# A delta-rule attention stage in 32 software-pipelined tiles: the order of its four engines rewritten

## The reference, cut to what matters

```python
xn = _ln(_layernorm(h), ln_in_g, ln_in_b)
k = xn @ Wk.T + 0.1 * modifier(xn)   # the same for v and q; modifier: 192 -> 48, gelu, -> 768
k, v, q = _ln(each, per head of 64)  # 12 heads
for t in range(64):                  # M: 64 x 64 per batch and head, 0 at first
    out_t = M @ q_t
    kn = k_t / (norm(k_t) + 1e-6)
    pred = M @ kn
    coef = pred + lr * (pred - v_t)
    M = M - outer(coef, kn)
h = h + sigmoid(x @ Wg.T + bg) * (out @ Wo.T)
h = h + _ln(Wo @ (W2 @ relu(W1 @ _layernorm(h))))   # the feed-forward part with its own Wo; biases left out
```

## Time and profile before

| | us |
|---|---|
| median of 3 runs | 1397.5 (1397.04 to 1405.56) |
| the profiled execution | 1401.61 |
| its span | 1399.8 |
| PE busy | 1234.2 (88%) |
| DVE busy | 816.8 (58%) |
| ACT busy | 625.8 (45%) |
| POOL busy | 612.0 (44%) |

### The profile page before, as it was taken

One profiled execution on the slowest core, in us unless ns is written; L12 is line 12 of the kernel. 1 busy time (PEld: TensorE's weight loads), 2 busy tenths in 40 slices (PEclk: granted clock), 3 DMA queues, 4 the chain that ended last, 5 costly groups with the idle time before them and its releaser, 6 DMA issues.

```text
span 1399.8 us, 45227 instructions
## 1 busy us (share of the span) xinstructions
PE 1234.2 (88%) x17572; PEld 1007.1 (72%) x17572; DVE 816.8 (58%) x2152; ACT 625.8 (45%) x1539; POOL 612.0 (44%) x721
## 2 busy tenths in 40 slices
PE   3879999999996569999999989999998999999874
PEld 3846666666664458788788878887887888888763
DVE  0173333333333246778768777876877777787652
ACT  0002222222222345666656656655665665666532
POOL 0000000000000364776677667567666766766621
PEclk9989999999997668999999999999999999999987
DMA  8859999999990001111111111111111111111110
GB/s 304 297 220 342 379 364 371 382 371 370 379 362 14 12 12 22 28 28 25 31 28 29 25 30 29 25 34 28 25 27 30 31 24 31 26 25 25 28 22 19
DMA packets 176410, 169.82 MB, mean 121 GB/s; under 512 B 118198, under 2 KB 146425, under 8 KB 175609
## 3 DMA queue, kind: packets, MB, share of 16 engines
q1 hardware_dynamic: 176234, 167.37, 37.0%
HBM read 154.72 MB, written 12.58 MB: 120 GB/s over the span
## 4 chain that ended last, share of the span: by engine, by line
PE 34%; POOL 32%; issue 17%; DVE 9%; DMA 3%; SPq 2%; ACT 2%; POOLq 0%; DVEq 0%; ACTq 0%
PE PS L435 29%; POOL region L1093 10%; POOL region L1074 4%; POOL region L1079 3%; POOL xr_lo L1098 2%; POOL region L1087 2%; POOL region L1050 2%; POOL region L1085 1%; POOL region L1054 1%; PE PS L504 1%; POOL region L1069 1%; POOL region L1057 1%; POOL region L1064 1%; PE PS L674 1%; DVE region L1447 1%
## 5 line engine op out<-in xcount | busy, mean ns | idle before, releaser
L435 PE MATMUL PS<-region 64*64 64x64 f32 (+5 forms) x5936 | 366.2, 288 | 46.5 <-DMA region<-in_w 23.2
L435 PEld LDWEIGHTS PS<-region 64*64 64x64 f32 (+3 forms) x5936 | 244.6, 140 | 145.1 <-issue 100.9
L1093 POOL TENSOR_TENSOR region<-region,powers 128x24 f32<-128x24 f32 x64 | 212.6, 3322 | 5.0
L1020 POOL TENSOR_TENSOR region<-region,powers 128x1 f32<-128x1 f32 x32 | 6.1, 192 | 417.5 <-DVE region L1201 417.5
L684 PE MATMUL PS<-region 64*64 64x64 f32 x4608 | 162.7, 226 | 2.3 <-ACT region L923 2.1
L684 PEld LDWEIGHTS PS<-region 64*64 64x64 f32 x4608 | 149.5, 141 | 21.0 <-issue 17.2
L1317 DVE TENSOR_REDUCE region<-region 128x12 f32<-128x768 f32 x96 | 91.0, 948 | 126.0 <-ACT region L895 126.0
L435 PE MATMUL PS<-cw_hi,xr_hi 128*128 128x512 f32 (+3 forms) x384 | 140.5, 366 | 10.0 <-POOL xr_lo L1098 10.0
L435 PE MATMUL PS<-cw_lo,xr_hi 128*128 128x512 f32 (+3 forms) x384 | 132.5, 345 | 0.0
L435 PE MATMUL PS<-cw_hi,xr_lo 128*128 128x512 f32 (+3 forms) x384 | 131.7, 343 | 0.0
L674 PE MATMUL PS<-region 64*64 64x64 f32 x3072 | 64.7, 232 | 63.8 <-DVE region L1336 31.4
...
## 6 DMA issues: line engine op xcount, KB each, us to landing
...
n_scratch<-region SPq DMA_DIRECT2D x256, 12.0 KB, 1.6
region<-i_scratch SPq DMA_DIRECT2D x256, 12.0 KB, 1.8
```

What stands on the lines that cost most here:

```text
L435: return nc.tensor.matmul(dst, lhsT, rhs, start=first, stop=last)
L1093: pool.tensor_tensor(rs[:, cols], rs_var[:, cols], root[:, cols], ALU.pow).then_inc(S["rs_ready"], 1)
```

## The change

It rewrites the order in the loops of all five engines, and some of what is in them:

- PE: `read_out` goes from the end of step k to the head of the next; only piece 0 stands ahead of `key_norms` and `grams`; `weigh_out` comes behind these; the pieces 3, 4 and 5 stand between links of the solve, with `gates` and the feed-forward part near the end. The PSUM banks are dealt anew (`PIECE_BANK`): pieces 3 to 5 use bank 7, which `weigh_out` fills too, so piece 3 now waits for `gated_ready`.
- ACT: the keys' squares come before `turned_out`, `mean_square(m)` behind piece 0.
- `head_rstds` takes k, q and v one by one (12 columns each) and has lost its multiplication by 1/64, which `squares` now does.
- v's sums, root and scaling (m = 2) are done at the head of the next step, as j.
- `low_part` moves from POOL to DVE.
- The inversion is done in one go at the end of DVE's step.
- `gather_blocks` stores n whole, in two DMAs of 64 partitions x 12 heads x 256 bytes, so that the diagonal blocks lie at a constant pitch, and reads them back as 96 x 16 runs of 64 bytes; before, it stored eight times 16 x 12 runs of 64 bytes and read 96 runs of 1 KB. On SP it comes before `store_result`.

```diff
+PIECE_BANK = (0, 1, 0, 7, 7, 7)
...
-                for b in range(NBLK):
-                    at = b % BPS * BLK
-                    sp.dma_start(n_dram[b].rearrange("h t j -> t h j"),
-                                 nmat[j % 2][b * BLK:b * BLK + BLK, :, at:at + BLK]).then_inc(S["n_stored"], 16)
-                sp.wait_ge(S["n_stored"], (j + 1) * NBLK * 16)
+                for e in range(2):
+                    rows = bass.AP(n_dram.tensor, e * BPS * BLK_PITCH, [[SEQ, SEQ], [HEAD_PITCH, HEADS], [1, SEQ]])
+                    sp.dma_start(rows, nmat[j % 2][64 * e:64 * e + 64, :, :]).then_inc(S["n_stored"], 16)
+                sp.wait_ge(S["n_stored"], (j + 1) * 32)
                 need(sp, "d_ready", j)
                 settled(sp)
-                sp.dma_start(blocks[:, :, :], n_dram.rearrange("b h t j -> (b h) t j")).then_inc(S["gather_done"], 16)
+                diagonal = bass.AP(n_dram.tensor, 0, [[BLK_PITCH, NBLK * HEADS], [SEQ, BLK], [1, BLK]])
+                sp.dma_start(blocks[:, :, :], diagonal).then_inc(S["gather_done"], 16)
...
+                if live(x + 2):
+                    need(sp, "x_ready", x + 1)
+                    settled(sp)
+                    load_h(hp, "hp_in", x + 2)
+                if live(j):
+                    gather_blocks(j)
                 if live(m):
                     store_result(m)
-                if live(j):
-                    gather_blocks(j)
...
+                    if i == 2:
+                        pe.wait_ge(S["raw_ready"], 6 * t + 1)
+                    if i == 3:
                         need(pe, "gated_ready", upto(t - 3))
-                    dst = PS[:, (0, 5, 1, 0, 1, 7)[i], 0:width]
+                    if i in (4, 5):
+                        pe.wait_ge(S["raw_ready"], 6 * t + i)
...
-            in_f, in_a, in_z = by_parity((0, 1)), by_parity((7, 0)), by_parity((1, 5))
+            in_f, in_a, in_z = by_parity((0, 1)), by_parity((0, 1)), by_parity((5, 2))
...
                     turn_kq(j)
                 if live(l):
-                    weigh_out(l)
+                    read_out(l)
                 if live(t):
-                    project(t, range(0, 3))
+                    project(t, range(0, 1))
                 if live(j):
                     key_norms(j)
                     grams(j, 0)
                     grams(j, 1)
+                if live(l):
+                    weigh_out(l)
+                if live(t):
+                    project(t, range(1, 3))
                 if live(x):
                     turn_x(x, j)
                 if live(t):
-                    project(t, range(3, 6))
+                    project(t, range(3, 4))
...
+                if live(t):
+                    project(t, range(4, 5))
...
+                if live(t):
+                    project(t, range(5, 6))
...
+                    ffn_first(l)
                     ffn_second(l)
-                if live(k):
-                    read_out(k)
...
-                act.activation(sq[:, m * KD:(m + 1) * KD], raw[:, m * KD:(m + 1) * KD], ACT.Square).then_inc(S["sq_ready"], 1)
+                act.activation(sq[:, m * KD:(m + 1) * KD], raw[:, m * KD:(m + 1) * KD], ACT.Square, scale=HD ** -0.5).then_inc(S["sq_ready"], 1)
...
+                if live(j):
+                    affine_kq(j)
+                    key_squares(j)
                 if live(l):
                     turned_out(l)
-                if live(j):
-                    affine_kq(j)
+                if live(t):
+                    take_piece(t, 0)
                 if live(m):
                     mean_square(m)
                 if live(t):
-                    take_piece(t, 0)
                     take_piece(t, 1)
+                    squares(t, 0)
                     take_piece(t, 2)
-                    squares(t, 0)
...
-                pool.tensor_tensor(ssm[:, cols], ssq[:, cols], per_head[:, cols], ALU.mult).then_inc(S["ssm_ready"], 1)
-                pool.wait_ge(S["ssm_ready"], 2 * t + i + 1)
-                pool.tensor_tensor(rs_var[:, cols], ssm[:, cols], eps[:, cols], ALU.add).then_inc(S["rs_var"], 1)
...
+            def head_rstds(t, m):
+                cols = slice(m * HEADS, (m + 1) * HEADS)
+                pool.wait_ge(S["ssq_ready"], 3 * t + m + 1)
+                pool.tensor_tensor(rs_var[:, cols], ssq[:, cols], eps[:, cols], ALU.add).then_inc(S["rs_var"], 1)
+                pool.wait_ge(S["rs_var"], 3 * t + m + 1)
+                if m < 2:
+                    need(pool, "kq_ready", 2 * (t - 1) + m + 1)
                 else:
                     need(pool, "vs_ready", t)
...
-            def low_part(x):
...
                 x, t, j, l, m = s, s - 1, s - 2, s - 4, s - 5
+                if live(j):
+                    head_rstds(j, 2)
                 if live(m):
                     output_rstd(m)
+                if live(x + 1):
+                    input_rstds(x + 1)
+                if live(j):
+                    key_lengths(j)
+                    scaled_mask(j)
                 if live(l):
                     residual_rstd(l)
-                if live(j):
-                    key_lengths(j)
+                if live(t):
+                    head_rstds(t, 0)
+                    head_rstds(t, 1)
...
+            def low_part(x):
+                dve.wait_ge(S["xr_hi"], x + 1)
+                need(dve, "piece_mm", 6 * x)
+                dve.tensor_tensor(xr_lo[:, :, :], x_aug[:, :, :], xr_hi[:, :, :].bitcast(F32), ALU.subtract).then_inc(S["xr_ready"], 1)
...
+                if live(j):
+                    moments(j, 2)
                 if live(m):
                     ffn_out(m)
                 if live(x + 1):
                     moments_h(x + 1)
                 if s == 0:
                     fold_weights()
+                if live(j):
+                    take_norm(j)
+                    take_a(j, 0)
+                    take_a(j, 1)
+                    scale(j, 2)
+                    inverse_norms(j)
+                if live(l):
+                    gate_and_add(l)
+                if live(j):
+                    take_n(j, 0)
+                    take_n(j, 1)
+                if live(t):
+                    moments(t, 0)
+                if live(k):
+                    take_e(k, 0)
+                    take_e(k, 1)
                 if live(l):
                     norm_h2(l)
                 if live(j):
+                    right_side(j)
                 if live(t):
+                    moments(t, 1)
+                if live(x):
+                    high_part(x)
+                    low_part(x)
+                if live(x + 1):
+                    normalise(x + 1)
                 if live(m):
                     result(m)
                 if live(t):
                     scale(t, 0)
                     scale(t, 1)
                 if live(j):
                     invert_small(j)
                     join(j, 4, 3).then_inc(S["sub_step"], 1)
+                    join(j, 8, 5).then_inc(S["d_ready"], 1)
```

143 lines of the change are left out of this document (45 added, 98 removed).

## The result

| | before | after |
|---|---|---|
| time, median of 4 runs each (range) | 1397.5 us (1397.0 to 1405.6) | 1505.6 us (1504.0 to 1508.0) |
| ratio, 95% interval | | 1.0752 (1.0724 to 1.0780) |
| span of the profiled execution | 1399.8 us | 1506.0 us |
| step: mean distance of `high_part`'s starts, 580 to 1300 us | 27.03 us | 31.03 us |
| granted clock, mean of the span | 0.95 | 0.91 |

The forecast was 1439 us in a range of 1392 to 1480: the sign was right, the time lies outside. Of the 108 us, some 42 were forecast and 66 were not. The step grew by 4.0 us where 1.5 were forecast; 28 x 4.0 = 112.

The account below looks back on a forecast made before the run. A ring across engines was taken as the bound, no engine full. PE's 24.67 + 2.7 + 0.6 gave 28.0, plus 0.5 for the clock 28.5 us a step against 27.01; over 28 steps +42: 1439 us, range 1392 to 1480.

Parts of the forecast that it names:

- What bounds the kernel: Kernel before: no engine full, the step is a ring over DVE, PE and ACT; 27.01 us against PE's own 24.67.
- What the change removes: DVE's 3.35 us wait for ACT's squares of v goes, as does PE's wait for take_e ahead of start_y.
- The wait in front of piece 3: PE reaches piece 3 at 10.3 us, waits for gated_ready behind POOL's key_lengths until 13.0: 2.7 us every step.
- first rival: POOL's ring is short and PE is the bound: 25.7 us a step, 1360 us; chance 0.11.
- The second wait: PE at ffn_second waits for ACT's relu, which stands behind both take_c: 0.6 us (0 to 0.9).
- A second ring gives the same.: DVE and POOL wait for each other, from v's moments over the roots and lengths to DVE's remaining work: 27.8 us.
- all that DVE does behind it: DVE's work behind inverse_norms in the second ring: 22.2 less 4.8 ahead of the wait, 17.4 us.
- At nothing: Low_part off POOL, 1/64 multiplications, split roots, later inverse, other banks, SP's order, later gates: all costed at nothing.
- The clock: PE's granted clock falls after long waits: 1.7 us lost in one earlier case; 0.5 us a step added (0 to 1.7).
- The gather: Two stores issue faster, the read has 1536 runs in place of 96; taken as just hidden before invert_small.
- the third rival: The read of 64-byte runs is late, DVE waits at invert_small: 29.8 us a step, 1476 us; chance 0.13.

Follow-up runs that it names:

- the loops open: Changed kernel with xr_hi/xr_lo double-buffered and key lengths first on POOL: 1348.6 us; also with the FFN's first product between third-order halves: 1338.8 us.
- both repairs together: Changed kernel with two buffers each for xr_hi and xr_lo, and key_lengths and scaled_mask ahead of POOL's other roots: 1348.6 us, ratio 0.9651.
- the run with two buffers: Changed kernel with two buffers each for xr_hi and xr_lo, so high_part need not wait for the current tile's last piece: 1433.4 us, ratio 1.0258.
- with POOL out of the loop: Changed kernel with key_lengths and scaled_mask ahead of POOL's other roots: 1489.3 us; with 16 unread transposes on PE ahead of key_norms added: 1411.3 us.

## Why the prediction was wrong, step by step

- *What bounds the kernel.* Right. The step was a ring and PE's own work 24.67 us; with the loops open the step comes down to 25.3 to 25.7.
- *What the change removes.* Right: `moments` of v no longer waits 3.35 us for ACT. That this is part of why both repairs together beat the kernel before is likely; no run has it alone.
- *The wait in front of piece 3.* Right in mechanism, as the run with two buffers shows. There, counted from `turn_kq` (940.28), POOL takes up `mean_square` at 5.6 us (5.7 forecast), the lengths end at 11.6 (11.6), piece 3 starts at 12.8 (13.0), and PE is there at 11.1 (10.3). PE waits 1.72 us at piece 3 in place of 2.7, and then 1.0 at `start_y`, or has the same in half-speed matmuls. That the totals agree so well, 28.84 us a step against 28.5 and 1433 against 1439 us, is in part luck: the 0.5 for the clock are in the sum, and the clock costs nothing there, while PE's own work is longer than the 24.67 us read from one step before (25.3: 25.74 with both loops cut, less 0.46 of wait). In the changed kernel the gate is open before PE comes in 21 of 32 steps. The prediction took that for a sign of its first rival, 1360 us; it came with 1506.
- *The second wait*, `ffn_second`: 0.46 us, 0.6 forecast.
- *"A second ring gives the same."* The terms held (6.6 us for 7.15 on POOL), but what stood in the sum as "all that DVE does behind it", 17.4 us without a wait, has one of 3.3 us in it, for PE. In the changed kernel this ring runs through `take_e`, `start_y`, piece 5 and `high_part`, not only through DVE and POOL, and it is the one that sets the step: 30.85 us in place of 27.8.
- ***"At nothing"* is the step that failed**: "The other bank changes, SP's order, `gates` later: all behind waits that are met long before." The prediction took piece 5's new place as a gain for PE and went through its consumers on PE and ACT, but never asked who waits for the piece to be *read*: `high_part`, which has no row of idle time in the trace before and so was not looked for. The inverse's place was weighed against `form_e` only, 14 us on; it is also ahead of v's sums on DVE, and so of all of POOL's roots, and of `ffn_out`, and that ahead of `key_norms`, which the change moved to where it meets it. Two edits costed at nothing closed one loop: 31.03 - 28.84 = 2.2 us a step, and 72 us by the run.
- *The clock.* 0.5 us a step was forecast, out of the 1.7 of the one long wait in the earlier trace rows. In the changed kernel and in the forecast's own state it costs nearly nothing, because other waits cover it; with POOL out of the loop it costs 2.9 us a step. A single price a wait was the wrong form.
- *The gather.* Right: hidden, and the DMA that the third rival (1476 us) feared lands in time; DVE waits for it in one step. The time lies nearer to that rival's than to the forecast, for another reason. Here the read of 1536 runs of 64 bytes lands 2.8 us after its issue (median; 1.9 with the old layout), and the price is under what shows. The Trainium skill (DMA: Bandwidth & Descriptors, Specifications) has transfers at line rate from 512 bytes on only; the 0.9 us go that way, and no run here shows what part of them is due to it.

Still open: why some steps of the changed kernel take 31.4 to 31.7 us and most 30.85. The longer ones have 7.1 to 7.4 us from v's sums to the lengths, or 9.0 to 9.1 from there to the end of `take_e`; what puts them there is not known. Open too is which single part of the change brings the 3.5% once the loops are cut. It was not tried, nor `key_norms` at its old place, behind pieces 1 and 2, which by the timeline would open the way over `ffn_out`; by the table the one over POOL would still hold the step.
